# Routed experts in tiles of two halves of 128 rows, each half with its own expert

## The chip, the cores and the metric

The kernel runs on one core of a Trainium2 chip. The metric is the device time of one execution in microseconds (us), as the median of several runs. TensorE is PE (its weight loads are PEld), VectorE is DVE, ScalarE is ACT, GpSimd is POOL, and SyncE is SP, which only issues DMAs.

## The reference, cut to what matters

The input x has 16 batches of 512 tokens with 256 features. One macaron block is computed: half a feed-forward step, attention, half a feed-forward step, each with a layer norm ahead of it.

```python
x = x + 0.5 * ffn(layernorm(x))
x = x + attention(layernorm(x))        # 16 heads of 16, ALiBi bias, forward and backward heads
x = x + 0.5 * ffn(layernorm(x))

def ffn(x):                            # flat: 8192 tokens of 256
    out = sum over 2 shared experts of (silu(x @ wg_s) * (x @ wu_s)) @ wd_s      # middle 128
    weights, indices = top_k(softmax(x @ router_w), 2)                           # 16 experts
    weights = weights / (weights.sum(-1) + 1e-9)
    for each token and each of its 2 experts e:
        out += weight * (silu(x @ wg_r[e]) * (x @ wu_r[e])) @ wd_r[e]            # middle 64
    return out
```

## The kernel before, in words

Each batch of a feed-forward step is normed, routed and run through the shared experts. For the routed experts its 1024 token copies are sorted by expert: POOL writes the normed rows with eight indirect DMAs (`scatter`) to `sorted_x` in DRAM, where each expert has a region of its own. The batches of each of the two layers (l = 0 ahead of the attention, l = 1 behind it) are put into groups: l = 0 has groups of 6 and 10 batches, l = 1 of 7, 6 and 3. When all batches of a group are sorted, DVE makes a table (`table`, L1512 to L1527) of the group's tiles: for each tile its expert and its first row. The counts are known only at run time, so the program has a fixed number of tiles, which is the largest number that can be needed: `n_tiles` = copies / 256 + 15, which is 39, 55, 43, 39 and 27 tiles, 203 in all. A tile that isn't needed reads a spare region. The rows from the end of an expert's copies up to a whole tile are filled with zeros by 16 DMAs for each group (`fill`, from a zeroed SBUF tile).

One tile, named T l g.j here, is 256 rows of one expert:
- SP loads its rows, 256 KB (`tile x`, L877 and L878), and the expert's weights, 256 KB (`tile weights`, L889 and L890): gate and up as 128x256, and down as 64x256, laid twice so that it stands on both halves of the partitions. For each of the two SP first reads a number of the table into a register (TENSOR_LOAD).
- PE transposes the rows (L1071), ACT copies them (L1276), PE multiplies by gate and up (L1081), ACT makes the tanh (L1282), DVE the product (L1619, L1624), PE multiplies by down (L1092), and ACT copies the result (L1291).
- The result goes to `sorted_y`: by SP (`tile put`, L895) in the three middle groups, by ACT (L1295) in the first and the last, which have more buffers for tiles (those of the attention, `p_buf`).
POOL then fetches the two results of each token (`fetch`, L1748), and DVE adds them (`combine`, L1637).

What each engine does and in which order is written out ahead by a planner (`Plan.run`): a list of pieces for each engine, each with a due time, a cost, what it needs and which buffers it takes. Every engine follows its list strictly, so a piece that waits holds all that stands behind it on its engine. The program's course: the feed-forward of batches 0 to 5; the tiles of the first group (T 0 0) with batches 6 to 9 of the feed-forward between them; then 64 attention pieces (16 batches of four heads-groups) with the middle groups' tiles and the feed-forward of l = 1 between them; at last the 27 tiles of the last group alone (T 1 2), and the fetches of the last batches. For the attention, SP also issues four `qk put` of each batch (L922), six DMAs each, and loads, puts and outputs of whole batches (L833, L838, L902, L907, L911).

## Time and profile before

| what | value |
|---|---|
| three runs | 2117.55, 2125.89, 2132.25 us; median 2125.89 us |
| the profiled execution's span, first to last instruction | 2171.8 us |
| PE busy | 1692.7 us, 78% of the span |
| DVE, ACT, POOL busy | 1481.6, 1041.9, 946.3 us |
| mean granted TensorE clock | 0.890 |
| DMA | 392.79 MB in 327978 packets |

The profiled execution has no time of its own beside its span. The span is 46 us (2.2%) over the median of the timed runs. Shares of busy time are a mean over stages, which are different; the stages have to be read one by one.

### The profile page before, as it was taken

Reading aid. Unit: us, or ns where it says so; the run is one execution under the profiler, and the core shown is the slowest. Engines: PE = TensorE matmul, PEld = TensorE weight load, DVE = VectorE, ACT = ScalarE, POOL = GpSimd, SP = SyncE. Lnnn points to the kernel's source line nnn. Section 1 sums busy time; section 2 is a strip of 40 time slices with the busy share of each in tenths; the row PEclk is TensorE's granted clock in tenths of the full one; section 3 lists DMA queues with packets and bytes.
Section 4 is the critical chain, followed back from the end, with each engine's and each line's share of the span. In section 5 each row is a group of like instructions: output and inputs, shape, how many; then the busy total and the mean of one; then the engine's idle time right before and its main releaser. Section 6 shows DMA issues by size and latency. Waiting matters only on the chain. (4 is left out here: it accounts for less than half of the span.)

```text
span 2171.8 us, 35275 instructions
## 1 busy us (share of the span) xinstructions
PE 1692.7 (78%) x10696; PEld 1120.9 (52%) x10696; DVE 1481.6 (68%) x3920; ACT 1041.9 (48%) x2263; POOL 946.3 (44%) x999
## 2 busy tenths in 40 slices
PE   3759885878898988798788898889878587894291
PEld 2646664545565655455455555646445255462261
DVE  4865656769776776788787776677777666573442
ACT  3325553445556655455455555555544244562061
POOL 1743337654524231654543533343454635135504
PEclk8879996899999999999898998989998688897696
DMA  7468862647878676746477867565465886865795
GB/s 209 138 196 269 262 200 92 147 103 208 223 184 246 170 220 150 167 97 127 113 182 182 219 157 193 136 177 152 101 129 136 242 239 164 220 189 167 240 331 159
DMA packets 327978, 392.79 MB, mean 181 GB/s; under 512 B 40296, under 2 KB 269032, under 8 KB 327784
## 3 DMA queue, kind: packets, MB, share of 16 engines
q1 hardware_dynamic: 260816, 267.81, 47.9%
q0 software_dynamic: 24576, 67.14, 11.0%
q10 hardware_dynamic: 42400, 55.59, 8.2%
q8 instruction: 88, 1.44, 0.3%
q14 instruction: 98, 0.80, 0.1%
HBM read 188.58 MB, written 155.19 MB: 158 GB/s over the span
## 5 line engine op out<-in xcount | busy, mean ns | idle before, releaser
L1325 ACT ACTIVATE p_buf<-bank 128x512 f32<-128x512 f32 x640 | 359.3, 599 | 231.4 <-PE bank L1165 166.3
L1566 DVE TENSOR_REDUCE row_max<-bank 128x1 f32<-128x512 f32 (+2 forms) x768 | 349.9, 503 | 120.7 <-PE bank L1148 103.1
L1782 POOL TENSOR_SCALAR_AFFINE_SELECT p_buf<-p_buf 128x512 f32<-128x512 f32 x256 | 160.3, 640 | 417.9 <-ACT p_buf L1325 415.6
L1132 PE MATMUL bank<-k_stack,q_stack 99*128 99x512 bf16 (+3 forms) x1024 | 251.7, 321 | 44.7 <-issue 31.9
L1165 PE MATMUL bank<-q_stack,k_stack 101*128 101x512 bf16 (+3 forms) x1024 | 240.4, 317 | 52.9 <-DMA q_stack<-shift_t 36.8
L1725 POOL DMA_INDIRECT sorted_x<-xn,position x224 | 220.8, 986 | 94.1 <-issue 52.5
L1748 POOL DMA_INDIRECT y_tok<-sorted_y,position x192 | 185.5, 966 | 150.2 <-DVE x_att L1637 45.7
L1185 PE MATMUL bank<-p_buf,v_rows 128*32 128x512 f32 (+3 forms) x2048 | 187.8, 467 | 27.7 <-POOL p_buf L1782 27.0
L1619 DVE SCALAR_TENSOR_TENSOR t_g<-t_th,bank 64x256 f32<-64x256 f32 x203 | 82.5, 407 | 163.2 <-ACT t_th L1282 146.3
L1291 ACT ACTIVATE t_y<-bank 128x256 f32<-128x256 f32 x406 | 133.3, 381 | 124.3 <-PE bank L1092 95.5
L1081 PE MATMUL bank<-t_xt,t_w 128*128 128x256 f32 x548 | 158.7, 416 | 35.9 <-DMA t_w<-expert_w 29.8
L1148 PE MATMUL bank<-cbf 128*128 128x256 bf16 (+1 forms) x640 | 170.7, 267 | 0.0
L1132 PEld LDWEIGHTS bank<-k_stack,q_stack 99*128 99x128 bf16 x1024 | 94.9, 103 | 137.2 <-issue 77.2
L1165 PEld LDWEIGHTS bank<-q_stack,k_stack 101*128 101x128 bf16 x1024 | 84.8, 101 | 155.5 <-issue 65.4
L1276 ACT ACTIVATE t_xt<-bank 128x512 f32<-128x512 f32 x203 | 118.6, 595 | 83.9 <-PE bank L1071 74.6
L974 PE MATMUL bank<-w_down,hs_buf 128*128 128x256 f32 x256 | 85.5, 334 | 68.9 <-POOL hs_buf L1755 39.5
L1081 PEld LDWEIGHTS bank<-t_xt,t_w 128*128 128x128 f32 x548 | 102.8, 203 | 68.6 <-DMA t_w<-expert_w 32.6
L1282 ACT ACTIVATE t_th<-bank 64x256 f32<-64x256 f32 x203 | 76.2, 375 | 128.3 <-PE bank L1081 108.1
L1667 DVE RECIPROCAL den<-den 128x128 f32<-128x128 f32 x128 | 109.3, 911 | 34.4 <-DMA den<-o_store 34.2
L1755 POOL TENSOR_TENSOR hs_buf<-h_buf,hs_buf 128x512 fp32r<-128x512 f32 x64 | 81.7, 1276 | 111.9 <-ACT hs_buf L1246 108.0
L1624 DVE TENSOR_TENSOR t_h<-bank,t_g 64x128 f32<-64x128 f32 x406 | 119.2, 294 | 13.3
L1092 PE MATMUL bank<-t_w,t_h 64*128 64x256 f32 x548 | 98.0, 434 | 14.0 <-DVE t_h L1624 8.4
(193 smaller groups left out, 3839.7 us busy)
## 6 DMA issues: line engine op xcount, KB each, us to landing
t_w<-expert_w SPq DMA_DIRECT2D x137, 256.0 KB
t_x<-sorted_x SPq DMA_DIRECT2D x137, 256.0 KB
sorted_y<-t_y SPq DMA_DIRECT2D x137, 256.0 KB
q_stack<-qk_part SPq DMA_DIRECT2D x192, 128.0 KB
k_stack<-qk_part SPq DMA_DIRECT2D x192, 128.0 KB
sorted_x<-zeros SPq DMA_DIRECT2D x69, 256.0 KB, 3.7
p_buf<-expert_w SPq DMA_DIRECT2D x66, 256.0 KB
p_buf<-sorted_x SPq DMA_DIRECT2D x66, 256.0 KB
```

What stands on the lines that cost most here:

```text
L1081: ins = pe.matmul(ps[:, 0:RT], weights[:, P * d:P * d + P], xt[:, d, :], start=(d == 0), stop=(d == ND - 1))
L1132: pe.matmul(ps[:, col:col + k1 - k0], q_stack[0:ROWS_S, h, P * qt:P * qt + P], k_stack[0:ROWS_S, h, k0:k1], start=(n == 0), stop=False, sk ...
L1148: ins = pe.matmul(dst, ident_bf, mask, start=False, stop=True, skip_group_check=True)
L1165: ins = pe.matmul(ps[:, col:col + q1 - q0], k_stack[0:ROWS_P, h, P * kt:P * kt + P], q_stack[0:ROWS_P, h, q0:q1], start=(n == 0), stop=Tru ...
L1185: ins = pe.matmul(ps[VR * hh:VR * hh + VR, q0:q1], v_rows[b % 2][:, v0:v0 + VR], p_of(u)[:, col:col + q1 - q0], start=(r == 0), stop=(r == 2),
L1291: act.activation(t_y[i][:, t, :], psum("ty", *of, t)[:, 0:D], ACT.Copy).then_inc(*ty_out.step(*of, t))
L1325: act.activation(p_of(u), psum("score", *of)[:, :], ACT.Exp).then_inc(*exp_done.step(*of))
L1566: ins = dve.tensor_reduce(row_max[g % 2][:, n:n + 1], src[:, col:col + q1 - q0], X, ALU.max)
L1624: dve.tensor_tensor(t_h[i][ME * t:ME * t + ME, :], ps[ME:P, at], t_g[:, at], ALU.mult).then_inc(*th_step.step(*of, "u", t))
L1725: pool.indirect_dma_start(sorted_x[l, group_of(l, b)], bass.IndirectOffsetOnAxis(ap=position[:, b, k, t:t + 1], axis=0), xn[buffer][:, t, ...
L1748: pool.indirect_dma_start(y[:, k, t, :], None, sorted_y[l, g], bass.IndirectOffsetOnAxis(ap=position[:, b, k, t:t + 1], axis=0)).then_inc( ...
L1782: pool.affine_select(blocks, blocks, [[0, GH], [1 if ahead else -1, P]], ALU.is_ge, zero, base=0, channel_multiplier=-1 if ahead else 1).t ...
```

## The change

A tile is still 256 rows, but its two halves of 128 rows each have an expert of their own. The table now counts in halves of 128 rows, so that an expert's copies are filled up to 128 rows rather than 256, and the fixed number of tiles falls: (copies / 128 + 16) / 2, which is 32, 48, 36, 32 and 20 tiles, 168 in all. Each half reads its own row of the table for its rows and for its expert: `tile x` is two loads of 128 KB, `tile weights` two loads of gate and up of 128 KB (`t_gu`) and two of down of 64 KB (`t_dn`; each lands only on the partitions of its half). The matmuls of gate and up take 128 columns of one half with that half's weights. Spare copies of down in the first and the last group lie in `o_pack` and `den`. Other tiles shared memory for this: `zeros` is now the start of `den`, two tiles that were apart lie in one, and the masks of the attention are held once rather than twice and read with a repeated dimension. The fill copies 128 rows from the spare rows (which are zero) to the end of an expert's copies, within DRAM, in place of 256 rows from SBUF. The planner's costs of the two SP pieces are raised from 0.8 and 0.9 to 1.5 and 2.3, which moves pieces on all engines.

```diff
+HT = RT // 2
...
-    return group_size(l, g) * S * 2 // RT + E - 1
+    return (group_size(l, g) * S * 2 // HT + E) // 2
...
-        part(at - 2.5, "SP", 0.8, x, *fills, *sent, *last,
+        part(at - 2.5, "SP", 1.5, x, *fills, *sent, *last,
...
-        part(at - (4.0 if many_tiles(l, g) else 2.5), "SP", 0.9, weights, (("table", l, g), "DVE"),
+        part(at - (4.0 if many_tiles(l, g) else 2.5), "SP", 2.3, weights, (("table", l, g), "DVE"),
...
-        t_w = [sb(f"t_w{i}", [P, ND * P + D]) for i in range(3)] + [p_buf[c][:, i, :] for c, n in ((1, 4), (2, 2))
-                                                                     for i in range(n)]
+        t_gu = [gu.rearrange("p (t n) -> p t n", t=2) for gu in [sb(f"t_gu{i}", [P, 2 * ND * P])[:, :] for i in range(3)] + [
+            p_buf[c][:, i, :] for c, n in ((1, 4), (2, 2)) for i in range(n)]]
+        t_dn = [sb(f"t_dn{i}", [P, D])[:, :] for i in range(3)] + [
+            o_pack[:, m, D * i:D * i + D] for m in range(2) for i in range(2)] + [den[:, D * i:D * i + D] for i in range(2)]
         t_xt = [sb(f"t_xt{i}", [P, ND, RT]) for i in range(2)]
-        t_th = sb("t_th", [ME, RT])
-        t_g = sb("t_g", [ME, RT])
+        t_tg = sb("t_tg", [P, RT])
...
         beyond = placed[:, :, :, :].rearrange("p k t e -> p (k t) e")
-        beyond_rows = sb("beyond_rows", [P, 2 * NT])
-        zeros = sb("zeros", [P, D])
+        beyond_rows = ranked[:, 0, 0:2 * NT]
...
-                return t[bass.ds(row, RT), :].rearrange("(i p) d -> p i d", p=P)
+                return t[bass.ds(row, HT), :]
...
+                    if (l, g) == ALL_GROUPS[0]:
+                        sp.wait_ge(spare_in, 16 * len(ALL_GROUPS))
                     for e in range(0, E, 2 if many_tiles(l, g) else 1):
                         row = sp.value_load(fill_i[0:1, e:e + 1])
-                        sp.dma_start(rows(sorted_x[l, g], row), zeros[:, :].unsqueeze(1).broadcast_to((P, 2, D))
-                                     ).then_inc(*filled.step(l, g, e))
+                        sp.dma_start(rows(sorted_x[l, g], row), rows(sorted_x[l, g], SPARE)).then_inc(*filled.step(l, g, e))
...
-                    row = sp.value_load(tile_i[l, g][j:j + 1, 1:2])
-                    sp.dma_start(t_x[i][:, :, :], rows(sorted_x[l, g], row)).then_inc(*tx_in[i].step(*of))
+                    for t in range(2):
+                        row = sp.value_load(tile_i[l, g][2 * j + t:2 * j + t + 1, 1:2])
+                        sp.dma_start(t_x[i][:, t, :], rows(sorted_x[l, g], row)).then_inc(*tx_in[i].step(*of, t))
...
+                            sp.wait_ge(spare_in, 16 * len(ALL_GROUPS))
                     if before["t_w", l, g, j]:
                         sp.wait_ge(*ty_full.at(*before["t_w", l, g, j][1:]))
-                    e = sp.value_load(tile_i[l, g][j:j + 1, 0:1])
-                    sp.dma_start(t_w[i][:, :], expert_w[bass.ds(e, 1)].rearrange("e p x -> p (e x)")
-                                 ).then_inc(*tw_in[i].step(*of))
+                    for t in range(2):
+                        e = sp.value_load(tile_i[l, g][2 * j + t:2 * j + t + 1, 0:1])
+                        at, both_d = slice(ME * t, ME * t + ME), ND * P
+                        sp.dma_start(t_gu[i][:, t, :], expert_w[bass.ds(e, 1), :, 0:both_d].rearrange("e p x -> p (e x)")
+                                     ).then_inc(*tw_in[i].step(*of, "hidden", t))
+                        sp.dma_start(t_dn[i][at, :], expert_w[bass.ds(e, 1), at, both_d:].rearrange("e p x -> p (e x)")
+                                     ).then_inc(*tw_in[i].step(*of, "out", t))
                 elif name == "tile put":
                     l, g, j = of
                     sp.wait_ge(*ty_out.at(*of, 1))
@@ -1064,7 +1073,7 @@
...
-                    weights, xt = t_w[w_home(l, g, j)], t_xt[index["t_xt", l, g, j]]
-                    for d in range(ND):
-                        ins = pe.matmul(ps[:, 0:RT], weights[:, P * d:P * d + P], xt[:, d, :], start=(d == 0),
-                                        stop=(d == ND - 1))
+                    weights, xt = t_gu[w_home(l, g, j)], t_xt[index["t_xt", l, g, j]]
+                    for t in range(2):
+                        at = slice(HT * t, HT * t + HT)
+                        for d in range(ND):
+                            ins = pe.matmul(ps[:, at], weights[:, t, P * d:P * d + P], xt[:, d, at],
...
-                        ins = pe.matmul(halves[t][:, 0:D], hidden[at, :], weights[at, ND * P:ND * P + D],
+                        ins = pe.matmul(halves[t][:, 0:D], hidden[at, :], weights[at, :],
...
-                        act.wait_ge(set_done, 4)
+                        act.wait_ge(spare_in, 16 * len(ALL_GROUPS))
                     for e in range(1, E, 2):
                         row = act.value_load(fill_i[0:1, e:e + 1])
-                        act.dma_start(sorted_x[l, g][bass.ds(row, RT), :].rearrange("(i p) d -> p i d", p=P),
-                                      zeros[:, :].unsqueeze(1).broadcast_to((P, 2, D))
+                        act.dma_start(sorted_x[l, g][bass.ds(row, HT), :], sorted_x[l, g][SPARE:SPARE + HT, :]
                                       ).then_inc(*filled_act.step(l, g, e))
...
-                done("whole", dve.tensor_scalar(count_i[:, :], n_of, 1.0 / RT, (RT - 1) / (2.0 * RT),
+                done("whole", dve.tensor_scalar(count_i[:, :], n_of, 1.0 / HT, (HT - 1) / (2.0 * HT),
                                                 ALU.mult, ALU.add))
                 done("tiles", dve.tensor_copy(tiles, count_i[:, :]))
...
-                done("skip", dve.tensor_scalar(left, tiles, -float(RT), float(CAP), ALU.mult, ALU.add))
+                done("skip", dve.tensor_scalar(left, tiles, -float(HT), float(CAP), ALU.mult, ALU.add))
```

On SP, in the first stretch of tiles, just ahead of the seventh row load; before, three instructions issue the weights of a tile, and three its rows:

```order
L889 TENSOR_LOAD tile_i
L890 ISA
L890 DMA p_buf<-expert_w 128x512
L877 TENSOR_LOAD tile_i
L878 ISA
L878 DMA p_buf<-sorted_x 128x2x256
L838 DMA x_store<-q_stack 128x4x256
```

On SP at about the same place in the changed program, where `den` holds the down weights:

```order
L881 TENSOR_LOAD tile_i
L882 ISA
L882 DMA p_buf<-sorted_x 128x256
L881 TENSOR_LOAD tile_i
L882 ISA
L882 DMA p_buf<-sorted_x 128x256
L895 TENSOR_LOAD tile_i
L897 ISA
L897 DMA p_buf<-expert_w 128x256
L899 ISA
L899 DMA den<-expert_w 64x256
```

The last four rows and the one ahead of them are the weights of one half only; they come again for the other half. A tile that had two loads of the table and two DMAs here has four and six.

On SP, the end of the program before; the last rows are the last weights' load, and then what is left of the outputs (`out`) and whole-batch loads (`gather`):

```order
L889 TENSOR_LOAD tile_i
L890 ISA
L890 DMA p_buf<-expert_w 128x512
L911 DMA out_dram<-x_ffn 128x4x256
L907 DMA x_ffn<-x_store 128x4x256
L911 DMA out_dram<-x_ffn 128x4x256 x2
```

The same end in the changed program:

```order
L881 TENSOR_LOAD tile_i
L882 ISA
L882 DMA p_buf<-sorted_x 128x256
L920 DMA out_dram<-x_ffn 128x4x256 x2
L916 DMA x_ffn<-x_store 128x4x256 x2
L920 DMA out_dram<-x_ffn 128x4x256
L916 DMA x_ffn<-x_store 128x4x256
L920 DMA out_dram<-x_ffn 128x4x256 x2
```

Two outputs and two loads that stood between the tiles' loads of the last group now stand behind all of them.

## Rows read from the trace of the kernel before

**Rows 1.** The page: the span.

```profile
span 2171.8 us, 35275 instructions
```

**Rows 2.** Stretches: us; PE, PEld, DVE, ACT, POOL busy; clock, DMA share, GB/s.

```profile
164.00:316.00 152.00, 135.58 (x783) 99.63 (x783) 93.45 (x294) 82.81 (x206) 54.54 (x53) 0.98 0.79 249
546.00:879.00 333.00, 296.45 (x1962) 193.47 (x1959) 233.98 (x603) 196.06 (x445) 113.05 (x123) 0.96 0.74 196
1090.00:1520.00 430.00, 378.72 (x2504) 243.66 (x2503) 319.63 (x812) 236.56 (x510) 178.01 (x193) 0.93 0.70 177
1737.00:1970.00 233.00, 196.98 (x1218) 126.04 (x1218) 147.34 (x369) 122.31 (x280) 76.33 (x84) 0.90 0.73 201
2062.00:2130.00 68.00, 60.77 (x316) 39.78 (x315) 30.23 (x89) 41.44 (x107) 0.00 (x0) 0.95 0.95 316
```

**Rows 3.** L1325 alone (attention's exp, ten to a piece) in four of these stretches.

```profile
546.00:879.00 333.00, 67.66 (x117) 0.96 0.74 196
879.00:1090.00 211.00, 61.11 (x113) 0.92 0.58 124
1090.00:1520.00 430.00, 100.38 (x177) 0.93 0.70 177
1737.00:1970.00 233.00, 40.12 (x70) 0.90 0.73 201
```

**Rows 4.** L1276 alone (one copy to each tile) in the stretches with tiles.

```profile
546.00:879.00 333.00, 32.38 (x55) 0.96 0.74 196
1090.00:1520.00 430.00, 24.97 (x42) 0.93 0.70 177
1737.00:1970.00 233.00, 22.42 (x38) 0.90 0.73 201
```

**Rows 5.** Timeline of PE, 204.5 to 209: start, us from first start to last end.

```profile
205.22 1.13 PE L1081 MATMUL bank<-t_xt,p_buf 128*128 128x256 f32 x4
206.19 1.04 PE L1071 MATMUL bank<-c,p_buf 128*128 128x128 f32 x8
```

**Rows 6.** Weight loads of L1071 (206 to 207) and L1081: ns min/median/max.

```profile
L1071 PEld LDWEIGHTS bank<-c,p_buf x8: 139/141/142, 206.0 to 206.8; 128*128 128x128 f32 x8
...
L1081 PEld LDWEIGHTS bank<-t_xt,t_w x548: 186/190/338, 546.4 to 1966.1; 128*128 128x128 f32 x183
```

**Rows 7.** Timeline of SP: first and last stretch of tiles; start, us.

```profile
133.05 0.37 SPq L890 DMA_DIRECT2D p_buf<-expert_w  x1
...
293.58 0.34 SPq L890 DMA_DIRECT2D p_buf<-expert_w  x1
...
2033.97 12.86 SPq L860 DMA_DIRECT2D sorted_x<-zeros  x8
...
2056.89 2.99 SPq L878 DMA_DIRECT2D p_buf<-sorted_x  x4
...
2118.41 1.61 SPq L890 DMA_DIRECT2D p_buf<-expert_w  x2
```

**Rows 8.** SP's instructions for one load and the puts: ns min/median/max.

```profile
L889 SPq TENSOR_LOAD <-tile_i x203: 12/285/1296, 132.4 to 2118.8; - x102
L890 SPq DMA_DIRECT2D t_w<-expert_w x137: 3/346/1878, 526.0 to 1960.9; - x137
L895 SPq DMA_DIRECT2D sorted_y<-t_y x137: 5/427/1362, 555.7 to 1970.0; - x137
L922 SPq DMA_DIRECT2D q_stack<-qk_part x192: 546/601/2081, 379.2 to 1870.9; - x192
```

**Rows 9.** SP's waits, 546 to 879: us in total, times, longest.

```profile
SPq L889 <- PE bank L1092: 67.1, 35, 7.6
SPq L877 <- PE bank L1071: 58.5, 29, 5.4
```

**Rows 10.** Timeline 2128 to 2134: the last tile's put, the first fetch after.

```profile
2129.79 0.37 ACTq L1295 DMA_DIRECT2D sorted_y<-t_y  x1
2132.74 0.94 POOL L1748 DMA_INDIRECT q_stack<-sorted_y,position  x1 [79.26 <-DMA sorted_y<-t_y]
```

More of the change, by code:

```diff
@@ L664, in build @@
         c32 = sb("c32", [P, P + NT * E + E + 2])
-        cbf = sb("cbf", [P, 7 * P], BF16)
+        cbf = sb("cbf", [P, 5 * P], BF16)
         bias_qk = sb("bias_qk", [P, 2, ND])
@@ L671, in build @@
         tile_no, tile_row = (c32[:, P + NT * E + E + i:P + NT * E + E + i + 1] for i in range(2))
-        ident_bf, mask_up, mask_low, earlier, ones_bf = (
-            cbf[:, P * i:P * j] for i, j in ((0, 1), (1, 3), (3, 5), (5, 6), (6, 7)))
+        ident_bf, mask_up, mask_low, earlier, ones_bf = (cbf[:, P * i:P * i + P] for i in range(5))
         xt_full, logits_full, route_full, rank_full = (signal(n) for n in (
@@ L1075, in do @@
                     l, g, j = of
-                    pe.wait_ge(*tw_in[w_home(l, g, j)].at(*of))
+                    pe.wait_ge(*tw_in[w_home(l, g, j)].at(*of, "out", 1))
                     pe.wait_ge(*tx_out.at(*of))
                     ps = take(("tgu", *of), th_step, *of, "u", 1)
-                    weights, xt = t_w[w_home(l, g, j)], t_xt[index["t_xt", l, g, j]]
-                    for d in range(ND):
-                        ins = pe.matmul(ps[:, 0:RT], weights[:, P * d:P * d + P], xt[:, d, :], start=(d == 0),
-                                        stop=(d == ND - 1))
+                    weights, xt = t_gu[w_home(l, g, j)], t_xt[index["t_xt", l, g, j]]
[3 more added lines that the diff above has]
+                            ins = pe.matmul(ps[:, at], weights[:, t, P * d:P * d + P], xt[:, d, at],
+                                            start=(t == 0 and d == 0), stop=(d == ND - 1), skip_group_check=True)
                     ins.then_inc(*tgu_full.step(*of))
@@ L1086, in do @@
                     pe.wait_ge(*th_step.at(*of, "u", 1))
-                    weights, hidden = t_w[w_home(l, g, j)], t_h[index["t_h", l, g, j]]
+                    weights, hidden = t_dn[w_home(l, g, j)], t_h[index["t_h", l, g, j]]
                     halves = [take(("ty", *of, t), ty_out, *of, t) for t in range(2)]
@@ L1819, in constants @@
     up, low = np.triu(np.full((P, P), neg), 1), np.tril(np.full((P, P), neg), -1)
-    cbf = np.concatenate([eye, up, up, low, low, np.triu(ones, 1), ones], 1).astype(bf16)
+    cbf = np.concatenate([eye, up, low, np.triu(ones, 1), ones], 1).astype(bf16)
     half = H // 2
```

20 lines of the change are left out of this document (10 added, 10 removed).

## The prediction

> **What bounds the kernel now.** I read the span first [rows 1], then the busy time by stretch [rows 2], because the stages differ, then what a tile costs in each, and last SP's timeline and waits, because the change gives SP more to issue than anybody else.
>
> The stretches tell three stories [rows 2]. Where attention runs with tiles between it (546 to 879, 1090 to 1520, 1737 to 1970) PE is busy 89%, 88% and 85% of the time at a granted clock of 0.90 to 0.96, so near its upper level of 2.4 GHz; DVE has 63% to 74%. PE is the bound there, with its order fixed. In the first stretch of tiles (164 to 316) PE has 89% and DMA 79%. In the last (2062 to 2130) DMA has 95% at 316 GB/s, and PE 89%: both are full.
>
> What a tile costs on the path can be read by comparing stretches. From 879 to 1090 no tile runs, and 113 exps are 11.3 pieces of attention in 211 us, 18.7 us each [rows 3]. From 546 to 879 there are 11.7 pieces and 55 tiles [rows 3, 4]: 333 - 11.7 x 18.7 = 114 us, 2.1 us a tile. From 1090 to 1520: 430 - 17.7 x 18.7 = 99 us for 42 tiles, 2.4 us. From 1737 to 1970: 233 - 7 x 18.7 = 102 us for 38 tiles, 2.7 us.
>
> SP is a strict queue. A load of rows comes every 0.87 us ((2.99 - 0.38) / 3 [rows 7]): 0.28 us for the number from the table, 0.35 to 0.38 us for the DMA [rows 8], and 0.2 us around them. The weights' load takes 0.85 us likewise, and a put 0.48. That is 1.7 us a tile in the first and last groups (where ACT puts) and 2.2 us in the middle ones. From 546 to 879 SP waits 126 of 333 us for PE to free a tile's buffers [rows 9]: it has room, about 40%.
>
> **The change part by part.**
>
> *Fewer tiles.* Seven fewer in each group. In the three attention stretches that saves 7 x (2.1 + 2.4 + 2.7) = 50 us if a tile still costs what it did. Nothing else covers PE's time there, so it comes off the end.
>
> *Matmuls of one tile.* Gate and up are eight instructions of 128 columns in place of four of 256. The four take 1.13 us, so one starts every 0.22 us or so [rows 5]; half the columns should take 0.11. The open cost is the weight load that each now needs: 190 ns at L1081 [rows 6]. The nearest row is L1071: eight f32 instructions of 128 columns, each with its own load of 141 ns, take 1.04 us together, one every 0.11 us [rows 5, 6]. Their loads are hidden although longer than that. Lower bound of the cost: 0. Upper: 190 - 110 = 80 ns for each of eight, 0.64 us a tile. I take 0, since L1071 is the same shape; the upper end is a rival.
> The Trainium skill ("TensorE: Matmul & The Clock Gate", The mechanism) says that a weight load overlaps running matmuls only when it is for other rows of the array. By that rule the eight loads of all 128 rows would stand open. The rows of L1071 speak against it.
>
> *SP's work.* Rows: two loads a tile, 1.7 us. Weights: for each half 0.85 us for the first DMA and 0.53 for the second (no table load: 0.35 for the DMA and the 0.2 around it), 2.7 us a tile. So 4.4 us a tile where it was 1.7, and 4.9 with the put where it was 2.2. This is the large price, and it lies beside other work only where SP has room:
> - 546 to 879: 48 tiles x 4.9 = 235 us, 12 qk puts of six DMAs at 0.65 us (0.60 [rows 8] and a gap) = 47, and 4 for whole batches: 286 us. The stretch would last 333 - 15 = 318 us. SP would be 90% full, in order, with waits on attention in it.
> - 1737 to 1970: 32 x 4.9 + 4 x 3.9 + 4 = 176 us of 214: 82%.
> - 1090 to 1520: 36 x 4.9 + 18 x 3.9 + 14 for fills + 5 = 265 us of 413: 64%, free.
> Late weights or rows stop PE. At 90% and 82% with three buffers each I give back 10 and 5 us of the 50; bounds 0 and 45 us.
>
> *First stretch.* SP's first weights leave at 133 and the last at 293.6 [rows 7]; the last result leaves at 317. Now SP needs 32 x 4.4 = 141 us, 12 us for its eight fills (they were slow: 12.86 us for the same eight in the last group [rows 7]), 5 for ten whole-batch DMAs and about 10 for loads that wait for a put to land: 168 us from 132, so 300; the rows come last now, and the tile then needs some 10 us more: 310. PE's work falls by 7 x 2.1 = 15 us, but the order has PE somewhat behind with batch 10 at that point, 5 us. SP takes the place of PE as the bound; I take 0, bounds -12 and +15.
>
> *Last stretch.* Nothing hides SP here. It starts at 2032 and must issue: tile 0's weights 2.7, fills 13, then 19 x 2.7 + 20 x 1.7 = 85 and one put: 2134. The last row load lands and is worked off in some 10 us (before, from the last weights' issue, 2118.41 + 1.61 = 2120.0 [rows 7], to the last result's put at 2129.79 [rows 10]): 2144, where it was 2130: +14 us, bounds +5 and +22. DMA would have room: 20 tiles move 896 KB each instead of 27 of 768, 18 MB for 21. The fetches behind it (from 2132.74 [rows 10]) stay as they are; the outputs and loads that moved behind SP's last tile have the first eight fetches, ten us, to hide in.
>
> *Fills.* 80 fills of 128 KB in place of 256 KB. Their issue costs the same on SP; DMA time falls, which could only matter at the start of the two outer stretches, within their bounds. The masks, the shared tiles and the table cost nothing: the same instructions with other addresses, and DVE's chain of steps for the logits was strictly ordered already.
>
> *Sum.* -50 + 15 + 0 + 14 = -21 us. The span is 2172 us against 2126 timed, and 2% of 21 us is nothing; so 2105 us from the median.
>
> **The rivals.**
>
> *SP stays hidden.* For it: SP's waits now are nearly all for buffers, and would simply be spent on issuing. Then the 50 us are kept whole, the first stretch gives back 12, and the last costs 5 to 14: about 2073.
>
> *SP is the bound wherever tiles run.* A list that waits for attention's buffers, for puts that land and for POOL can't be full. If SP can use only 80% of its time in the mixed stretches, they take 286 / 0.8 = 357 us (+24 where it was 333), 176 / 0.8 = 220 (-13), 413 (-17), the first 151 / 0.8 = 189 and 10 of tail from 132: 331 (+14), and the last +20. That is +28 us: 2154. The point from which it decides is a usable share under 0.85 in 546 to 879. For it: six qk puts' DMAs stand behind late tile loads, and PE's attention behind both.
>
> *Weight loads stand open.* 0.64 us x 116 tiles of the three attention stretches = 74 us on PE: -50 + 74 + 14, and the first stretch +8: 2172. The rule of the Trainium skill named above would give this or more. L1071 makes it improbable.
>
> *The tiles are not worth their measured price*, because PE waits for something else in their place (DVE at 74% from 1090 on): half of the 50 us is lost, and the sum is near 0: 2130.
>
> **How the numbers follow.** The forecast with its bounds has 0.45, SP hidden 0.2, SP the bound 0.18, open loads 0.05, tiles worth half 0.12. The likeliest gives 2105 us. From 2068 to 2152 all but some 2 in 10 is held: it reaches to SP hidden and to SP the bound, and leaves the open loads out. A change of 1% (21 us) is about what a measurement of this kernel can tell from none. The forecast stands on that line: half of its 0.45 is faster by over 1%, and all of SP hidden, and little of the rest: 0.46. Within 1%: 0.34. Slower: SP as the bound and open loads, 0.20.
>
> **What would show it.** Right: eight instructions of gate and up in about 1.1 us; SP with hardly a wait for PE's buffers in the first and last stretch, row and weight loads back to back there at 4.4 us a tile; the last group's tiles to end at about the same distance from its table as computed (112 us where it was 98); DMA share in it well under 0.95; the three attention stretches shorter by 5 to 17 us each. Wrong: PE waiting for `t_gu`, `t_dn` or `t_x` for more than 10 us in each stretch, or attention's rows waiting for a late qk put; a clock that falls in the outer stretches because PE waits more, which would make its tiles longer; a second DMA of SP that costs less or more than 0.53 us.

## The result, and the profile after

The changed kernel takes 2247.7 us (median of 4 runs, 2246.4 to 2258.1) against 2129.1 us before: a ratio of 1.057, 95% interval 1.053 to 1.061. I had forecast 2105 us with a range of 2068 to 2152. The sign is wrong, and the time lies outside the range.

The profiled execution of before is 2.2% longer than the median, so its stretches can't be set against those of after directly. I compare with mm8 instead, an experiment below that is the kernel before with another cut of four matmuls: 2128.8 us against 2131.3 of before, ratio 1.000 (0.997 to 1.003), span 2124.0. Its line numbers are those of before, or two higher.

The stretches of the changed kernel, which answer to [rows 2] (us; PE, PEld, DVE, ACT, POOL busy; clock, DMA share, GB/s):

```profile
156.00:329.00 173.00, 129.62 (x792) 102.58 (x791) 81.84 (x263) 71.51 (x174) 44.22 (x43) 0.88 0.68 211
597.00:960.00 363.00, 291.40 (x2038) 197.61 (x2039) 223.26 (x574) 186.19 (x418) 108.44 (x118) 0.90 0.73 189
1218.00:1592.00 374.00, 322.87 (x2289) 215.86 (x2288) 277.33 (x691) 206.17 (x445) 161.67 (x174) 0.93 0.70 177
1786.00:2021.00 235.00, 184.10 (x1241) 123.60 (x1240) 139.44 (x348) 110.56 (x251) 78.27 (x86) 0.88 0.77 204
2075.00:2200.00 125.00, 72.75 (x344) 53.29 (x344) 38.69 (x117) 33.75 (x82) 20.98 (x21) 0.69 0.67 205
```

Roughly the same stretches of mm8, by what happens in them (in the second it has 55 tiles and 121 exps, the changed kernel 48 and 116):

```profile
155.00:307.00 152.00, 136.48 (x951) 107.54 (x948) 95.73 (x300) 84.61 (x211) 55.83 (x54) 0.99 0.79 251
536.00:874.00 338.00, 303.89 (x2205) 211.18 (x2198) 239.02 (x611) 198.99 (x451) 115.51 (x126) 0.95 0.73 198
1133.00:1507.00 374.00, 331.62 (x2385) 224.44 (x2386) 280.72 (x702) 214.31 (x468) 162.29 (x175) 0.95 0.68 176
1706.00:1931.00 225.00, 190.91 (x1377) 131.55 (x1375) 143.43 (x369) 122.92 (x282) 76.49 (x84) 0.95 0.76 212
2005.00:2082.00 77.00, 64.96 (x442) 49.66 (x440) 34.72 (x99) 42.81 (x108) 5.17 (x5) 0.92 0.96 329
```

But for POOL in the last stretch (17% against 7%) no engine is busier than in mm8: PE falls from 90% to 80% in the second stretch, DMA from 0.96 to 0.67 in the last. Something that these rows don't count has become the bound: SP, which only issues. Its instructions answer to [rows 8] (ns min/median/max):

```profile
L881 SPq TENSOR_LOAD <-tile_i x336: 262/278/1787, 150.6 to 2190.4; - x168
L882 SPq DMA_DIRECT2D t_x<-sorted_x x232: 332/333/1586, 587.0 to 2005.0; - x116
L897 SPq DMA_DIRECT2D t_gu<-expert_w x232: 327/339/957, 588.7 to 2013.9; - x116
L899 SPq DMA_DIRECT2D t_dn<-expert_w x232: 474/475/1377, 589.3 to 2014.4; - x116
```

And SP's timeline in the last stretch (start, us; answers to [rows 7]):

```profile
2150.83 0.34 SPq L897 DMA_DIRECT2D p_buf<-expert_w  x1
2151.36 0.47 SPq L899 DMA_DIRECT2D o_pack<-expert_w  x1
2152.32 0.34 SPq L897 DMA_DIRECT2D p_buf<-expert_w  x1
2152.84 0.47 SPq L899 DMA_DIRECT2D o_pack<-expert_w  x1
...
2155.95 1.16 SPq L882 DMA_DIRECT2D p_buf<-sorted_x  x2
2157.61 0.33 SPq L897 DMA_DIRECT2D p_buf<-expert_w  x1
```

One half's weights take 2152.32 - 2150.83 = 1.49 us, the two row loads 2157.61 - 2155.95 = 1.66: 4.6 us a tile, back to back. From the last exp of attention to the last tile's copy 20 tiles take 177 us, where 27 took 153 in mm8 (rows below). Summed from its instructions, with gaps under 0.08 us, SP is in use for 90, 87, 70, 85 and 88% of the five stretches; in mm8 for 53, 52, 43, 50 and 76%. Its waits for a tile's buffers, 126 us in the second stretch of before and 141 in mm8, have fallen to 35 from 597 to 960 (answers to [rows 9]):

```profile
SPq L895 <- PE bank L1103: 26.9, 9, 6.3
SPq L881 <- PE bank L1080: 7.6, 3, 3.0
```

and PE waits in SP's place, first in that stretch, then from 2105 to 2200:

```profile
PE bank L1092 <- DMA t_dn<-expert_w: 21.6, 8, 11.0
PE bank L1143 <- DMA k_stack<-qk_part: 10.7, 1, 10.7
PE bank L1080 <- DMA t_x<-sorted_x: 10.1, 4, 3.4
...
PE bank L1080 <- DMA p_buf<-sorted_x: 22.7, 16, 3.6
```

The second of these is attention's. SP issued the twelve DMAs of this `qk put` and the one before it from 882.0 to 890.3, and PE waited until 902.3: they took 12 us to land, with the DMA engines full (a share of 0.97 to 1.15 from 885 to 905). That they left late because tile loads stood ahead of them in SP's list is likely, but not measured.

Where the time went, by two lines of each trace: attention's exps (640 of them) and the copies of the tiles' results, each with its first and last start. First the changed kernel, then mm8:

```profile
L1333 ACT ACTIVATE p_buf<-bank x640: 572/597/694, 449.7 to 2022.3; 128x512 f32<-128x512 f32 x160
L1299 ACT ACTIVATE t_y<-bank x336: 357/382/441, 162.9 to 2199.3; 128x256 f32<-128x256 f32 x168
```

```profile
L1327 ACT ACTIVATE p_buf<-bank x640: 572/597/678, 403.4 to 1928.8; 128x512 f32<-128x512 f32 x160
L1293 ACT ACTIVATE t_y<-bank x406: 357/380/440, 159.2 to 2081.7; 128x256 f32<-128x256 f32 x136
```

| piece of the span | mm8 | changed | difference |
|---|---|---|---|
| to the first exp | 403.4 | 449.7 | +46 |
| first to last exp (the mixed stretches) | 1525.4 | 1572.6 | +47 |
| last exp to the last tile's copy | 152.9 | 177.0 | +24 |
| to the end | 42.3 | 46.1 | +4 |

The sum is +121 us (2245.4 - 2124.0). The same four pieces are read of every run below.

### The profile page after: what moved, and what is told of

The parts are those of the page before. It is cut to its first block and busy times, and to the rows that moved or that the text cites. A ratio compares the mean times of both kernels' runs of the same rounds, so it can differ in the third digit from the quotient of the medians.

```text
span 2245.4 us, 37328 instructions
## 1 busy us (share of the span) xinstructions
PE 1665.7 (74%) x10948; PEld 1133.5 (50%) x10948; DVE 1444.7 (64%) x3815; ACT 993.2 (44%) x2123; POOL 945.9 (42%) x999
## 5 line engine op out<-in xcount | busy, mean ns | idle before, releaser
L1627 DVE SCALAR_TENSOR_TENSOR t_tg<-t_tg,bank 64x256 f32<-64x256 f32 x168 | 69.7, 415 | 181.3 <-ACT t_tg L1290 177.7
L1092 PE MATMUL bank<-t_xt,t_gu 128*128 128x128 f32 x928 | 141.7, 301 | 53.1 <-DMA t_dn<-expert_w 45.0
L1092 PEld LDWEIGHTS bank<-t_xt,t_gu 128*128 128x128 f32 x928 | 127.1, 210 | 74.7 <-DMA t_dn<-expert_w 51.8
L1299 ACT ACTIVATE t_y<-bank 128x256 f32<-128x256 f32 x336 | 110.5, 382 | 120.6 <-PE bank L1103 97.2
L1284 ACT ACTIVATE t_xt<-bank 128x512 f32<-128x512 f32 x168 | 99.9, 596 | 132.9 <-PE bank L1080 123.8
L1290 ACT ACTIVATE t_tg<-bank 64x256 f32<-64x256 f32 x168 | 63.1, 376 | 188.1 <-PE bank L1092 161.7
L1777 POOL TENSOR_TENSOR qk_part<-rest,qk_part 128x512 bf16<-128x512 f32 x64 | 74.3, 1164 | 103.5 <-ACT qk_part L1315 103.3
L1632 DVE TENSOR_TENSOR t_h<-bank,t_tg 64x128 f32<-64x128 f32 x336 | 98.7, 294 | 10.9
```

The source lines that it names most:

```text
L1092: ins = pe.matmul(ps[:, at], weights[:, t, P * d:P * d + P], xt[:, d, at], start=(t == 0 and d == 0), stop=(d == ND - 1), skip_group_check ...
L1299: act.activation(t_y[i][:, t, :], psum("ty", *of, t)[:, 0:D], ACT.Copy).then_inc(*ty_out.step(*of, t))
```

## The experiments

Medians are given with the ratio to before of the same session, whose median lay between 2120 and 2131 us.

**The order alone, and the order taken back.**

```diff
# cost_only: the kernel before with
-"SP", 0.8, x ... "SP", 0.9, weights
+"SP", 1.5, x ... "SP", 2.3, weights
# old_cost: the changed kernel with the reverse
```

> The kernel before with one edit: the planner's costs of the two SP pieces raised from 0.8 and 0.9 to 1.5 and 2.3, as the change does. Tiles, DMAs and bytes are those of before, so only the order of the pieces on all engines moves. Theory S (SP's own issue work, 4.6 us a tile where it was 1.7, is what costs the time): the order is innocent, within 1% of before, 2129 plus or minus 20 us. Theory O (the order that the new costs give is what costs, as the start-up suggests, where attention's first exp came 34 us later although the tiles ended only 12 us later): a good part of the 119 us shows here already, 2160 to 2230 us.

> The changed kernel with the planner's two costs put back to 0.8 and 0.9, nothing else. Theory O: most of the loss goes, 2130 to 2190 us, and the start-up falls back by some 20 us. Theory S: SP's work per tile is unchanged, so the time stays at 2230 to 2270 us, or gets worse since the planner now believes SP to be free when it is not.

cost_only: 2153.2 us, ratio 1.015 (1.008 to 1.021). old_cost: 2244.0 us, 1.058 (1.052 to 1.064), 4 us from the change. In the change the order is worth nothing in all: its first exp comes at 433 us in place of 450, and 15 us more in the mixed stretches and 3 behind them are the price. In the kernel before the costs do lose 1.5%, a loss of the planner's order alone. Theory O is out as the cause of the 119 us, but an order is worth more than my text ever said.

**SP's work taken away, and given back without bytes.**

```diff
# w_only: the changed kernel with
-for t in range(2): read the expert; DMA of gate and up (128 KB); DMA of down (64 KB)
+read the expert of half 0; one DMA of 256 KB
# w_old: w_only with the planner's costs 0.8 and 0.9
# w_pad7: w_only with seven more register reads per tile
# w_tiny: w_only, and behind each tile's weights
+spare_e = sp.value_load(tile_i[l, g][2 * j + 1:2 * j + 2, 0:1])
+for k in range(3):
+    sp.dma_start(scratch[at + k:at + k + 1, :], expert_w[bass.ds(spare_e, 1), k, 0:64])
# w_split: w_only with the 256 KB in three DMAs, 128 + 64 + 64 KB
```

> The changed kernel, its order, its 168 tiles, its two row loads and its eight matmuls of 128 columns kept, but with one number read and one DMA of 256 KB for a tile's weights in place of two numbers and four DMAs (2 x 128 KB and 2 x 64 KB). What it leaves out: the second half's own expert; both halves use the weights of the first. The fills are of 256 rows again, still within DRAM. SP issues some 2.6 us a tile less work by two thirds of 2.97 us, that is about 2.6 us a tile instead of 4.6. Theory S: the last stretch of tiles, 94 us for 20, falls to about 20 x 2.6 + 20 = 70 us, and the whole to 2130 to 2170 us. Theory O, or a theory that the eight weight loads of PE or the two row loads cost the time: hardly any change, 2220 to 2250 us. A theory of bytes (weights 384 KB a tile, now 256) also gives a gain, but only where the DMA share is near its top, which is none of the stretches after the change (0.67 to 0.73): under 20 us.

> w_only with the planner's two costs back at 0.8 and 0.9 (leaves out the second half's own expert, as w_only). The costs alone made the kernel before 33 us slower and made no difference to the change. Theory O2 (the raised costs give a worse order, which shows only where SP isn't the bound): 2050 to 2070 us. Otherwise: as w_only, 2080 to 2100 us.

> The run with one weights DMA per tile (w_only), and seven more reads of a table number into a register in front of each tile's weights, on SP, used for nothing. It leaves out what w_only leaves out (the second half's own expert). A read took 0.28 us in the trace of the change and some 0.03 us around it, so SP gets 2.1 us more per tile and is where the change had it (4.6 us), while bytes, packets and every DMA stay those of w_only. Theory S (issue work of SP, whatever it consists of): all of the 160 us between w_only (2088) and the change (2248) comes back: 2230 to 2270 us. Theory B (64-partition DMAs, 1 KB pieces, late landing of the fourth DMA): it stays near 2090 to 2120 us.

w_only: 2088.3 us, ratio 0.983 (0.976 to 0.991). w_old: 2082.9 us, 0.978 (0.972 to 0.984). In all, the order makes no difference here either, though its pieces move: w_old has its first exp 14 us earlier and takes 18 us more from first to last exp (1499.8). The register reads of w_pad7 aren't in its program: its trace has 568 TENSOR_LOADs, as w_only's. So it is w_only again (2094.5 us) and says nothing on SP; I take 2091 for the two. One DMA and one read for a tile's weights in place of four and two are worth 157 us, far more than I expected. But bytes and pieces fell with SP's work; w_tiny parts them.

> The run before this with extra register reads told nothing: its program holds the same 568 reads as w_only, since unused reads are dropped. Here w_only (second half's own expert left out) gets, behind each tile's weights DMA, one more read of a table number and three DMAs of 256 bytes that use it, from DRAM to a scratch place in DRAM that nobody reads. Nobody waits for them. That is as many SP instructions as the change has, with next to no bytes: by the DMAs' 0.34 to 0.52 us each and the rest of the rhythm some 2 us a tile. Theory S (the time SP needs to issue): 2230 to 2270 us, the whole 160 us come back. Theory B (what the DMAs move and when the last of them lands): 2085 to 2110 us. Between them: both have a share, to be read off in proportion.

w_tiny: 2259.8 us, ratio 1.066 (1.058 to 1.074). All of it is back, with 0.8 KB a tile. SP in its last stretch:

```profile
2120.00 0.33 SPq L897 DMA_DIRECT2D p_buf<-expert_w  x1
2120.82 1.85 SPq L902 DMA_DIRECT2D scratch<-expert_w  x3
2123.16 1.15 SPq L884 DMA_DIRECT2D p_buf<-sorted_x  x2
2124.80 0.33 SPq L897 DMA_DIRECT2D p_buf<-expert_w  x1
```

4.8 us a tile, where w_only has 2.5. The two lines of w_only, then of w_tiny:

```profile
L1329 ACT ACTIVATE p_buf<-bank x640: 575/597/691, 409.7 to 1891.9; 128x512 f32<-128x512 f32 x160
L1295 ACT ACTIVATE t_y<-bank x336: 360/380/440, 164.9 to 2038.6; 128x256 f32<-128x256 f32 x168
```

```profile
L1336 ACT ACTIVATE p_buf<-bank x640: 572/597/686, 453.5 to 2025.7; 128x512 f32<-128x512 f32 x160
L1302 ACT ACTIVATE t_y<-bank x336: 359/382/458, 166.6 to 2211.5; 128x256 f32<-128x256 f32 x168
```

The first and the middle piece of w_tiny are within 4 us of the changed kernel's (453.5 and 1572.2), the third is 9 us longer (185.8). Nobody waits for the tiny DMAs, and they don't slow the loads: a weights load lands 3.3 us after its issue, in w_only 3.5 (medians). What they take is SP's time. This settles the cause of the loss: the issue work of SP.

> w_only with its 256 KB of weights in three DMAs, as the change cuts them: gate and up on 128 partitions (128 KB), and down as two of 64 partitions (64 KB each); one number read. Second half's own expert left out. Bytes are those of w_only, the pieces have 1 KB instead of 2 KB as in the change, and SP has two more issues a tile: 0.5 us each, so 2.6 + 1.1 = 3.7 us. Theory S, on the straight line from w_only (2088) to the change (2248, 2 us more): +85 us, 2175 us. Theory B with the pieces' size as the cause: nearly all of it, 2230. Bytes as the cause: 2090 to 2110 us.

w_split: 2161.9 us, ratio 1.016 (1.013 to 1.019). With the bytes of w_only and 3.8 us of SP a tile it lies where a line from 2.5 us (2091) to 4.8 us (2260) puts 3.8 us: 2187 us, less 25. The 25 us lie outside the mixed stretches: from first to last exp w_split has 1531.7 us, 50 more than w_only for 116 x 1.3 = 151 us of SP, 0.33 per us, and w_tiny 90 more for 267 us, 0.34. So pieces of 1 KB and DMAs of 64 partitions add nothing beyond SP's time.

**Where it costs.** The tiny DMAs in the middle groups alone, and in the first and last alone.

```diff
# tiny_mid, tiny_out: w_tiny, its four added instructions under
+if not many_tiles(l, g):        # tiny_mid
+if many_tiles(l, g):            # tiny_out
```

> w_only (second half's own expert left out) with the read and three tiny DMAs of 2.35 us a tile on SP in the three middle groups alone (116 tiles). All 168 tiles with it cost 170 us over w_only (2088 to 2260). By my prediction's view the mixed stretches have room on SP and only the last has none: 2100 to 2120 us. By the spans of w_tiny against w_only (from attention's first exp to the last piece 1533 us against 1448) they carry 85 us: 2165 to 2180 us. If it is a question of the part of SP that is used, no stretch under 0.7 loses anything, and the third stretch (0.77 in w_tiny) little.

> The same in the first and the last group alone (52 tiles). By the spans of w_tiny against w_only: the first exp comes 44 us later and the last tile is done 44 us later than the end of attention would give (225 us from batch 15's second half to the last tile, against 181): 2165 to 2180 us. Nearly all of SP's extra 122 us would then be on the path, 70% of it. By my prediction, which gave the first stretch 0 and the last +14 for 2.7 us a tile: 2100 to 2110 us.

tiny_mid: 2191.9 us, ratio 1.031 (1.025 to 1.036). tiny_out: 2182.4 us, 1.026 (1.022 to 1.031). The two lines of tiny_mid, then of tiny_out:

```profile
L1337 ACT ACTIVATE p_buf<-bank x640: 573/597/674, 412.9 to 1995.5; 128x512 f32<-128x512 f32 x160
L1303 ACT ACTIVATE t_y<-bank x336: 360/380/445, 167.2 to 2143.3; 128x256 f32<-128x256 f32 x168
```

```profile
L1337 ACT ACTIVATE p_buf<-bank x640: 572/597/685, 452.6 to 1947.9; 128x512 f32<-128x512 f32 x160
L1303 ACT ACTIVATE t_y<-bank x336: 360/382/445, 165.6 to 2132.7; 128x256 f32<-128x256 f32 x168
```

tiny_mid has the middle piece at 1582.6 (+100 over w_only) and nothing elsewhere over 4 us. tiny_out has +43 before the first exp, +38 in the last group, +13 between. Per us of SP's work added: outer groups 52 x 2.35 = 122 us of SP cost 91 us, 0.75; middle groups 116 x 2.35 = 273 us cost 101, 0.37. (The two lose 192 us together, w_tiny 169, so they don't add up exactly.) The mixed stretches lose as much as the outer ones, though SP isn't full there: from the first to the last result's copy of each middle group it is in use for 88, 71 and 85% of the time. PE is stopped by late loads, from 561 to 912 by 19.8 us for rows and 15.4 for weights, and once by a `qk put`, 13.5 us.

**The change's other parts, on the kernel before.**

```diff
# x_two: each tile's rows by two reads and two DMAs of 128 rows
+for t in range(2):
+    row = sp.value_load(tile_i[l, g][j:j + 1, 1:2])
+    sp.dma_start(t_x[i][:, t, :], sorted_x[l, g][bass.ds(row + P * t, P), :])
# mm8: gate and up as eight matmuls of 128 columns
+for t in range(2):
+    for d in range(ND):
+        pe.matmul(ps[:, at], weights[:, P * d:P * d + P], xt[:, d, at], ...)
# dram_fill: 256 rows filled from the spare rows, within DRAM
+sp.dma_start(sorted_x[l, g][bass.ds(row, RT), :], sorted_x[l, g][SPARE:SPARE + RT, :])
```

> The kernel before with each tile's rows loaded by two DMAs of 128 rows, each with its own read of the number, in place of one of 256 rows. Same bytes and pieces of 1 KB, 0.82 us more of SP for each of 203 tiles (2.6 and, with the put, 3.1 us). Theory S with a threshold: SP has room here (it is used to 52% in the second stretch and 41% in the third), so only the last stretch, where the DMA engines bound it, could feel it: 2125 to 2150 us. Theory S as a straight line (80 us per us): +65 us, 2195 us.

> The kernel before with gate and up computed as eight matmuls of 128 columns in place of four of 256, with the same weights; nothing else. The rival that their weight loads stand open: 0.64 us for each of 203 tiles where PE is the bound, up to +80 us (some 2200). My own value, cost nothing: within 1%, 2110 to 2140 us. In the traces the eight took 301 ns each with the waits of their first in it, against 416 for four, which can't tell.

> The kernel before with only its fills changed: 256 rows copied within DRAM from the spare rows in place of 256 rows from a zeroed SBUF tile. In the change a fill's DMA takes SP 0.52 us where it took 0.37, 80 of them, so +12 us of SP in all, but the eight fills of the last group came every 1.6 us before and may come faster. Theory: nothing that can be told, 2115 to 2140 us. If copies within DRAM disturb the tiles' loads: 2140 to 2160 us.

x_two: 2154.1 us, ratio 1.012 (1.010 to 1.015): 203 x 0.82 = 166 us of SP cost 26 us, 0.16 per us. That is 4 us above the threshold theory and 41 under the straight line. Its two lines:

```profile
L1326 ACT ACTIVATE p_buf<-bank x640: 572/597/685, 411.1 to 1936.9; 128x512 f32<-128x512 f32 x160
L1292 ACT ACTIVATE t_y<-bank x406: 356/380/445, 159.1 to 2105.0; 128x256 f32<-128x256 f32 x136
```

From first to last exp it has 1525.8 us, as mm8 (1525.4): the 137 x 0.82 = 112 us of SP in the middle groups cost nothing, with SP in use for 65, 53 and 64% of these groups' stretches (first to last copy; mm8 52, 44 and 52%). The loss is outside, 8 us ahead of the first exp and 15 behind the last, where SP is in use for 87% of the last group's stretch. So there was free room in the mixed stretches. It is used up by the time of w_split, with 83, 62 and 75%, where a microsecond of SP costs 0.33.

mm8: 2128.8 us, 1.000 (0.997 to 1.003): the eight weight loads cost nothing. The Trainium skill ("TensorE: Matmul & The Clock Gate", The mechanism) has weight loads overlap running matmuls only for other rows of the array; 203 x 4 more loads of all 128 rows that leave the time where it was speak against that rule in this use. The same section also has a load into the background weight buffer pulled ahead of running matmuls, and with that sentence they agree. dram_fill: 2133.6 us, 1.0035 (1.001 to 1.006), 7 us if one takes it at its word.

**SP relieved, with the output kept.**

```diff
# act_half: half 1's read and two DMAs issued by ACT (a buffer list of its own)
+part(at - ..., "SP", 1.3, weights, ...);  part(at - ..., "ACT", 1.5, weights, ...)
# one_dma2: one DMA of 256 KB for each half
+sp.dma_start(t_w[i][:, t, :], expert_w[bass.ds(e, 1)].rearrange("e p x -> p (e x)"))
+t_w=2 in place of 3, wide_w=4 in place of 6
# one_aput: one_dma2, and ACT puts the tiles' results in all groups
```

> The changed kernel with the second half's weights (one number read, two DMAs) issued by ACT instead of SP; the planner's cost of SP's weights piece is 1.3 and ACT's is 1.5. Bytes, DMAs and PE's work are those of the change; only the engine that issues half of the weights changes. Theory S: SP's share falls from 4.6 to 3.1 us a tile, ACT (49% busy) takes 1.5 us a tile; the last stretch falls from 94 to some 75 us, the whole to 2170 to 2210 us. Theory B (bytes and packets of the extra weight DMAs): no gain, 2240 to 2260 us. Against both: ACT stands in PE's way with a wait for a weights buffer, then it is slower than the change in the mixed stretches while the last stretch is still shorter.

> The changed kernel with one DMA of 256 KB for each half's weights (gate, up and down together, on all partitions) in place of two; SP's work per tile is 1.64 for the rows and 1.64 for the weights, 3.3 us in place of 4.6. To have room, weights have two buffers in place of three in the middle groups and four in place of six in the first and last, and the planner's cost of the weights piece is 1.5. Bytes per tile rise from 896 to 1024 KB (rows, weights and put). Theory S, by a straight line between w_only (2.6 us, 2088) and the change (4.6 us, 2248): 2.6 + 0.7 gives 2144 us; in the last stretch 20 tiles take 20 MB, some 65 us at the 316 GB/s that it had before. Against: two buffers are too few, then PE waits for weights and SP for PE's release: 2160 to 2220 us.

> The change with one 256 KB DMA for each half's weights (one_dma2, 2160 us) and the results of the middle groups' tiles put by ACT right behind its own copies, as in the first and last group, in place of SP (the planner's costs are those of the first and last group). SP loses 0.58 us and a wait for ACT for each of 116 tiles. Theory S: by the slope of 80 us per us of SP and tile (160 us for 2.0 us on all 168 tiles), 0.6 us on 116 of them gives -33 us: 2125 us, level with before. If ACT's issue stands in attention's way as it did when it issued weights (act_half), no gain: 2150 to 2180 us.

act_half: 2221.0 us, 1.046 (1.040 to 1.052). A third of SP's tile work gone brings 27 us, where the line gives some 110: ACT's list is as strict as SP's. From 582 to 937 SP is down to 65%, but this is the time in which ACT stood ahead of its copies, its own issuing included ("issue" is time in which it waited for nothing that the profile shows):

```profile
ACT t_y L1319 <- issue: 98.6, 41, 5.6
```

one_dma2: 2159.9 us, 1.015 (1.009 to 1.021), against a line value of 2150 for its 3.3 us. With two buffers PE waits for weights from 568 to 918:

```profile
PE bank L1087 <- DMA t_w<-expert_w: 38.5, 16, 6.3
```

one_aput: 2179.3 us, 1.023 (1.019 to 1.026), 19 us worse than one_dma2: less on SP and more on ACT, and the same 38.8 us of waits for weights. Here ACT is the worse place for a DMA in the middle groups.

**Fewer tiles without more of SP.** Of a group's halves all that pair up are put into whole tiles again, and the last eight tiles take the rest.

```diff
# mix: the changed kernel with
+def n_whole(l, g): return group_size(l, g) * S * 2 // RT
+if j < n_whole(l, g): one read and DMA of 256 rows, one read and DMA of 256 KB of weights
+else: two of each, a weights buffer for each half
# table: a row and an expert for the whole tiles, and for the 16 halves left
# find: y = x row - sum([row >= region + CAP] * drop) + sum([row >= thr] * more)
# mix3: fewer waits in table and find; the planner counts 6.0 and 1.8 for them
# mix3b: mix3 with the planner's SP costs 1.5 and 2.3 (1.15 for a half)
```

> A version of the change that computes the reference with 168 tiles but gives SP little more than before: of each group's tiles all but eight are whole again (256 rows of one expert, one row load and one weights DMA, 1.7 us of SP), and only the last eight have two halves with an expert each (the halves that don't pair up, and what is left over), where each half's weights are one DMA of 256 KB into a buffer of their own (3.3 us). SP's work for tiles is 128 x 1.7 + 40 x 3.3 = 350 us, as before (203 x 1.7 = 345), where the change has 773 and w_only 415. The table takes DVE some 24 more small steps for each group and finding a result's row four more for each batch. If fewer tiles are worth what w_only (2088) and its copy with the old costs (2083) say: 2080 to 2105 us, faster than both. If DVE's longer chains at the start of the first and last group and in the 32 finds cost as much: 2110 to 2130 us.

> mix (2151 us) with DVE's extra steps made cheaper: the table's 36 steps wait only for what they need, with independent ones between, and a find has one wait less; the planner counts 6.0 and 1.8 us for the two, in place of 2.7 and 1.15. All the rest is as in mix: 168 tiles, the last eight of a group in halves. If DVE's chains are what mix lost against w_only: 2105 to 2130 us. If they aren't, and the 36 finds and 5 tables cost by the order alone or not at all: 2140 to 2155 us.

> mix3 with another order: the planner counts 1.5 us for a tile's rows and 2.3 for its weights (1.15 for each half's), as the change and w_only have it, though SP needs 0.8 each. Only the order of the pieces differs from mix3. In the kernel before these costs lost 33 us, in the change and in w_only they made no difference; so if an order is worth so much by itself, mix3 and mix3b differ by 10 to 40 us, either way, and one number of a version says little about what its edit is worth; if not, they agree within 10 us.

mix: 2150.9 us, ratio 1.010 (1.007 to 1.014), above both of its ranges. SP is in use for 51, 54, 47, 53 and 63% of the five stretches (from 160, 560, 1150, 1720 and 1990), about as in mm8, so its loss against w_only doesn't come from SP. DVE has more to do, 237 and 290 us in these two stretches (74% and 81%; mm8 had 71% and 75%), since a table takes 10 us in place of 3 and a find 2.1 in place of 1.1:

```profile
560.00:880.00 320.00, 277.12 (x1817) 181.86 (x1814) 237.47 (x588) 176.78 (x396) 110.45 (x120) 0.93 0.71 191
1150.00:1510.00 360.00, 307.16 (x2115) 197.93 (x2116) 290.39 (x720) 199.52 (x427) 151.77 (x164) 0.94 0.68 169
```

That DVE is what mix lost isn't shown: mix3b does the same arithmetic, its DVE is busy for 75 and 78% of about the same stretches (580 to 908, 1162 to 1529), and it is 43 us faster.

mix3: 2138.9 us, 1.003 (1.001 to 1.005), between its two ranges. mix3b: 2107.5 us, 0.987 (0.984 to 0.991). **mix3b beats both kernels**: 1.3% under before and 6.2% under the change (2107.5 / 2247.7). Its two lines:

```profile
L1354 ACT ACTIVATE p_buf<-bank x640: 573/597/685, 416.2 to 1905.4; 128x512 f32<-128x512 f32 x160
L1320 ACT ACTIVATE t_y<-bank x336: 358/380/406, 169.0 to 2061.5; 128x256 f32<-128x256 f32 x168
```

Between first and last exp it has 1489.2 us, 36 less than mm8. But its whole lead over mix3, 31 us, is order alone, and more than its lead over before, 22 us; that fewer tiles gain is shown better by w_old against x_two, which have the same planner costs and the same SP work a tile (71 us). Why that order is the better one is open.

## Why the prediction was wrong

**What holds.** *A tile's worth.* Fewer tiles were to save 50 us in the mixed stretches. w_only has them with 2.5 us of SP a tile: 1482.2 us from first to last exp against 1525.4 in mm8, 43 us less. x_two has 203 tiles at 2.5 to 2.6 us of SP, 2154 us; w_only and w_old, with 168, are 63 to 71 us below it. So the gain is there, but its size in the mixed stretches moves with the order: w_old has 26 us less than mm8 (both with the costs 0.8 and 0.9), w_only 69 less than cost_only (both with the raised ones). The rival that halved the 50 us isn't excluded; it would explain 25 us of a miss of 142. *The matmuls.* Cost nothing, as taken: mm8. *SP's work per tile.* Forecast 4.4 us, measured 4.6. The second DMA of a half costs SP 0.67 us without the read (1.49 - 0.82), where I took 0.53, since a DMA to 64 partitions takes 475 ns and not 0.35 us. *The fills*, nothing or 7 us.

**What failed: the price of SP's work.** The forecast was -21 us, measured against mm8 +121. Of the 142 us between them 82 lie in the mixed stretches (-35 forecast, +47 measured), 46 ahead of the first exp, 10 between the last exp and the last copy, and 4 behind it. The step for the mixed stretches read "at 90% and 82% with three buffers each I give back 10 and 5 us of the 50; bounds 0 and 45 us". Measured: w_only's 1482.2 us become 1572.6, so 90 us are given back (with the other order, from w_old to old_cost, 88). The work itself was nearly right: in the second stretch SP issued for 314 us, where I had 286. Wrong was that work under 100% of a stretch is nearly all hidden work. SP's list is strict and depends on PE's releases, and PE's on SP's loads. In the mixed stretches added work cost nothing up to 65% (x_two), but 0.33 us per us at 62 to 83% (w_split) and 0.37 at 71 to 88% (tiny_mid): a price that begins well below a full queue. I had read 126 us of waits in [rows 9] as 126 us of room. Part of them was (x_two spent 45 us there, 55 x 0.82, without loss); the rest was the lead that SP kept over PE. The third stretch, which I called free at 64%, is at 70%. From the first to the last copy of its group the change takes 365 us, w_only 347, and mm8, with seven tiles more, 356: it lost its gain too.

**The first stretch** was taken at 0, bounds -12 and +15. It costs 46 us to the first exp. The last tile's copy of that group comes 22 us later than in mm8, beyond the bound: SP is in use for 155 of 173 us there, with hardly a wait. Against the profile of before, from which I had the 317 us, it is only 12 us (329.1). The other 10 us are the greater length of that profile, 316.8 where mm8 has 306.9, which the sum called nothing. The other 24 us of the 46 lie between this copy and the first exp, 120 us in place of 96. SP's work isn't their cause, for w_only has 120 us there too (289.5 to 409.7). Most of it is the order: old_cost and w_old, with the old costs, have 102 us. I had costed no order at all. What SP's work costs is seen from w_only to the change, +40 us, all of it ahead of that copy, and from w_only to tiny_out, +43 us for 2.35 us a tile.

**The last stretch** was taken at +14, bounds +5 and +22. It is +24 to the last copy. SP issues back to back as forecast; 0.2 us more a tile are 4 us of it. Another 9 us are again the length of the profile of before, which has 161.5 us from last exp to last copy where mm8 has 152.9. Its two lines:

```profile
L1325 ACT ACTIVATE p_buf<-bank x640: 571/597/685, 415.6 to 1967.9; 128x512 f32<-128x512 f32 x160
L1291 ACT ACTIVATE t_y<-bank x406: 357/380/445, 166.3 to 2129.4; 128x256 f32<-128x256 f32 x136
```

In its own terms the step came out: the end at 2144 was 176 us behind that profile's last exp (1967.9), and 177.0 were measured. PE got slower beside it: while the group's tiles run the granted clock is 0.73 of 2.4 GHz in the mean (2115 to 2199), against 1.00 in mm8 (2022 to 2082), so much of the stretch is at the lower level of 1.2 GHz. A tile's eight matmuls take 2.07 us at 2152, where the clock is 0.50, and 1.13 at 2160, where it is back at 0.91:

```profile
2152.02 2.07 PE L1092 MATMUL bank<-t_xt,p_buf 128*128 128x128 f32 x8
...
2160.79 1.13 PE L1092 MATMUL bank<-t_xt,p_buf 128*128 128x128 f32 x8 [0.20 <-issue]
```

and the two stretches around them, with the columns of the stretches above (the clock is the third number from the end):

```profile
2150.00:2155.00 5.00, 4.95 (x20) 3.57 (x20) 0.42 (x2) 1.64 (x5) 0.00 (x0) 0.50 0.63 177
2159.00:2163.00 4.00, 2.71 (x16) 1.93 (x16) 0.85 (x3) 2.17 (x6) 0.00 (x0) 0.91 0.65 202
```

This hardly held SP up: from 2105 to 2200 SP waits 0.5 us in all for PE to free a tile's buffers. So little of the 24 us can be the clock's; a run that parts it from the rest is lacking.

**The rivals.** "SP is the bound wherever tiles run" was the right mechanism, at a chance of 0.18 and 2154 us. Its point of decision, a usable share of SP under 0.85, was wrong: SP was used to 0.87 there and the loss was four times the rival's (119 us against 28). It priced only the time by which SP's work overruns a stretch, and none of the waits on late loads inside it. Nor did the range take in what its own bounds were blind to: the largest one, 45 us given back in the mixed stretches, was half of the 90 that came, and no term stood for the order.

## What to carry to other kernels

Cost an issuing engine as any other: instructions per tile times their measured time, 0.8 us for a number read and a DMA, more for 64 partitions. Its waits for released buffers are in part its lead, not free room: here it went from 52 to 65% of a mixed stretch for nothing, and paid a third of a microsecond for each one added on the way to 83%. Before a change doubles its work, put tiny DMAs in its queue and read the price of a microsecond there. If a finer cut saves work on one engine but multiplies the DMAs, cut finely only where it pays: here eight tiles of a group.

An order written by a planner is worth 1.5% either way by itself here (cost_only +33 us, mix3 to mix3b -31 us), so compare an edit in more than one order before its size is believed.

## What the runs showed of the hardware

A DMA's issue time on SP hangs on its shape and not on its bytes (medians): 333 ns for 128 rows of 1 KB from DRAM to 128 partitions and as much for 128 rows of 2 KB (256 KB, w_only), 475 ns for 64 KB to 64 partitions, 0.49 us for 256 bytes within DRAM (x504, 1.85 us for three), 0.52 for 128 KB within DRAM. The smallest was among the dearest.
